# Transposes moved ahead of filler matmuls, and key and value tiles that rotate singly over seven PSUM banks, in a one-core hybrid block

## The reference

```python
t = t + _L2_ffn_ref(_ln_t(t), router_w, router_b, expert_w, expert_b)   # mixture of experts
t = t + _L3_attn_ref(_ln_t(t), mask, wq_w, wq_b, wk_w, wk_b, ...)       # linear attention, 16 heads of 32
t = t + _L3_ffn_ref(_ln_t(t), sigma, phi, M_u, ...)                     # spectral layer
```

## Time and profile before

| | us |
|---|---|
| median of 3 runs | 213.16 |
| lowest and highest run | 212.28 and 216.89 |
| span of the profiled execution | 211.0 |
| its busy time, PE | 179.3 |
| its busy time, DVE | 154.0 |
| its busy time, ACT | 97.4 |

### The profile page before, as it was taken

The page is one execution under the profiler, slowest core; times in us unless marked ns, Lnnn a source line. Parts: engine busy times, 40 slices in busy tenths (PEclk is TensorE's granted clock), DMA queues, the critical chain, the costliest instruction groups (busy, mean ns, idle before and its releaser), DMA issues.

```text
span 211.0 us, 7008 instructions
## 1 busy us (share of the span) xinstructions
PE 179.3 (85%) x3059; PEld 132.5 (63%) x3067; DVE 154.0 (73%) x347; ACT 97.4 (46%) x240; POOL 39.2 (19%) x57
## 2 busy tenths in 40 slices
PE   7799989798999987993688899768589979978994
PEld 2677669798998987931234677325245827646872
DVE  2789998959899999969877455598668757647201
ACT  2743998386889869422011351120758620016200
POOL 5971000004404413450100300332100000120000
PEclk9999999999999999999999999999965899999999
DMA  6930346344457530000044021001210072000000
GB/s 185 289 118 5 89 151 199 102 158 149 151 160 207 158 95 0 7 1 2 10 155 123 20 65 55 0 0 28 69 33 0 6 173 45 0 0 3 3 0 25
DMA packets 9203, 16.03 MB, mean 76 GB/s; under 512 B 2536, under 2 KB 3912, under 8 KB 9044
## 3 DMA queue, kind: packets, MB, share of 16 engines
q1 hardware_dynamic: 9028, 15.28, 24.4%
q10 hardware_dynamic: 144, 0.30, 0.4%
HBM read 15.15 MB, written 0.42 MB: 74 GB/s over the span
## 4 chain that ended last, share of the span: by engine, by line
PE 48%; DVE 32%; issue 8%; ACT 7%; POOL 2%; DMA 2%; POOLq 1%; DVEq 0%
PE ps L1547 46%; DVE onehot L1075 5%; DVE dots L1101 2%; POOL rstd L583 2%; DVE arena L455 2%; DMA cst<-in_cst 2%; DVE att L1125 1%; DVE arena L440 1%; ACT arena L646 1%; DVE stu_fq L1450 1%; ACT onehot L842 1%; ACT table L646 1%; ACT arena L863 1%; ACT arena L730 1%; DVE dots L1107 1%
## 5 line engine op out<-in xcount | busy, mean ns | idle before, releaser
L1547 PE MATMUL ps<-table,onehot 128*128 128x64 bf16 x1728 | 52.4, 193 | 5.6 <-DVE onehot L1075 2.9
L1547 PEld LDWEIGHTS ps<-table,onehot 128*128 128x128 bf16 x1728 | 51.3, 98 | 6.9 <-issue 4.0
L1547 PE MATMUL ps<-spare 128*128 128x512 bf16 (+1 forms) x120 | 31.4, 385 | 9.8 <-DVE rexp L1366 2.3
L730 ACT ACTIVATE arena<-ps 128x512 f32<-128x512 f32 (+1 forms) x40 | 21.3, 553 | 13.8 <-PE ps L1547 13.7
L455 POOL TENSOR_TENSOR arena<-arena,w4p 128x288 f32<-128x288 f32 x21 | 16.2, 802 | 58.2 <-DVE arena L455 58.0
L1547 PEld LDWEIGHTS ps<-spare 128*128 128x128 bf16 x128 | 11.2, 102 | 22.9 <-issue 2.8
L583 POOL TENSOR_TENSOR rstd<-var_eps,cst 128x4 f32<-128x4 f32 (+2 forms) x9 | 8.8, 982 | 80.5 <-DVE var_eps L944 54.6
L1547 PE MATMUL ps<-arena 128*32 128x66 f32 (+6 forms) x388 | 22.1, 277 | 0.2 <-DVE arena L1327 0.2
L646 ACT ACTIVATE arena<-ps 128x512 f32<-128x512 f32 (+4 forms) x17 | 7.2, 465 | 31.2 <-PE ps L1547 25.5
L1547 PEld LDWEIGHTS ps<-arena 128*32 128x32 f32 (+3 forms) x388 | 18.3, 146 | 4.3 <-issue 1.6
L1075 DVE TENSOR_SCALAR onehot<-indexb,cst 128x2304 bf16<-128x2304 bf16 (+1 forms) x24 | 17.7, 770 | 0.0
(11 more groups left out here) (280 smaller groups left out, 306.9 us busy)
## 6 DMA issues: line engine op xcount, KB each, us to landing
indexb<-index_rows SPq DMA_DIRECT2D x20, 288.0 KB, 3.5
stu_fq<-index_rows SPq DMA_DIRECT2D x8, 288.0 KB, 3.4
arena<-in_toep SPq DMA_DIRECT2D x2, 514.0 KB, 5.9
l<-in_l SPq DMA_DIRECT2D x1, 646.5 KB
stu_fq<-in_stu SPq DMA_DIRECT2D x1, 560.0 KB, 3.7
onehot<-in_l3w SPq DMA_DIRECT2D x1, 512.0 KB
table<-stu_mixed SPq DMA_DIRECT2D x4, 128.0 KB, 2.2
l<-in_l SPq DMA_DIRECT2D x1, 384.0 KB, 7.0
```

Of the source, the lines that this page charges most:

```text
L730: nc.scalar.activation(gv[:, b % 2, :, at:at + count, :], ps[:, SB[n % len(SB)], 0:count * SLOT].rearrange("p (s a d) -> p a s d", s=count ...
L1547: return nc.tensor.matmul(out_ap, lhsT, rhs, start=start, stop=stop)
```

## The change

Mixture: the four fillers behind `eps1` go, and each half is turned, copied and multiplied before the next half is turned, with one filler behind each transpose. The wait for the expert weights' load moves ahead of the first transpose.

Linear attention: the three fillers behind `x41` and the three behind `cen1` go; two fillers with no wait of their own stand ahead of the first transpose. Bank 0 (`ROWBANK`) holds both transposes. The sixteen key and value tiles rotate over the other seven banks in the order in which they are read, so `v3` takes the bank that `fk0` frees, `k4` that of `vs0`, `v4` that of `fk1`, and so on: each waits for a single step. `turn1` comes right behind `v2`, and its copy `rows1` stands on ACT behind `vc0`. `queries(0)` waits for no step for image 0, and for `vs4`, `fk5`, `vs5` for the others.

```diff
-        t4 = Steps(sem("tensor_moe"), "turn0 turn1 experts0 experts1 sum")
+        t4 = Steps(sem("tensor_moe"), "turn0 experts0 turn1 experts1 sum")
...
-        a5 = Steps(sem("scalar_linear"), "rows0 ek0 vc0 ek1 vc1 ek2 vc2 ek3 rows1 vc3 " + " ".join(f"ek{t} vc{t}" for t in range(4, T))
+        a5 = Steps(sem("scalar_linear"), "rows0 ek0 vc0 rows1 " + " ".join(f"ek{t} vc{t}" for t in range(1, T))
...
-        t5 = Steps(sem("tensor_linear"), "turn0 k0 k1 k2 k3 v0 v1 v2 v3 turn1 k4 k5 v4 v5 k6 k7 v6 v7"
+        t5 = Steps(sem("tensor_linear"), "turn0 k0 k1 k2 k3 v0 v1 v2 turn1 v3 k4 v4 k5 v5 k6 v6 k7 v7"
...
-        KBANK, VBANK = (lambda t: 2 * t % 8), (lambda t: (2 * t + 1) % 8)
+        KBANK, VBANK, ROWBANK = (6, 1, 3, 5, 7, 2, 4, 6), (7, 2, 4, 6, 1, 3, 5, 7), 0
...
-                if t == 3:
-                    rows_copied(t5, a5, 1, VBANK(0))
                 act.wait_ge(t5.sem, t5[f"v{t}"])
...
+                if t == 0:
+                    rows_copied(t5, a5, 1, ROWBANK)
...
             occupied_after(v3, ("x3", 4), bank=6)
-            occupied_after(v4, ("var0", 4), ("eps1", 4), bank=6)
-            turned_rows(v4, t4, 0, 4)
-            occupied(1, 6)
-            turned_rows(v4, t4, 1, 5)
+            occupied_after(v4, ("var0", 4), bank=6)
             pe.wait_ge(d_moe, 5 * 16)
             for h in range(NH):
+                turned_rows(v4, t4, h, 4 + h)
+                occupied(1, 6)
                 pe.wait_ge(a4.sem, a4[f"rows{h}"])
...
-            tile_biases(range(B), KBANK, WK, stop=False)
-            occupied_after(v4, ("x41", 3), bank=7)
+            tile_biases(range(B - 1), KBANK, WK, stop=False)
+            pe.wait_ge(v4.sem, v4["x41"])
+            tile_biases([B - 1], KBANK, WK, stop=False)
             tile_biases(range(B - 1), VBANK, WV, stop=False)
-            occupied_after(v5, ("cen1", 3), bank=7)
-            turned_rows(v5, t5, 0, 7)
+            occupied(2, ROWBANK)
+            turned_rows(v5, t5, 0, ROWBANK)
             pe.wait_ge(a5.sem, a5["rows0"])
             tile_products("k", range(B), KBANK, WK, start=False)
-            tile_biases([B - 1], VBANK, WV, stop=False)
-            tile_products("v", range(B), VBANK, WV, start=False)
-            pe.wait_ge(v5.sem, v5["vs0"])
-            turned_rows(v5, t5, 1, VBANK(0))
-            for pair in ((4, 5), (6, 7)):
-                for name, bank, w, freed in (("k", KBANK, WK, "fk"), ("v", VBANK, WV, "vs")):
-                    pe.wait_ge(v5.sem, v5[f"{freed}{pair[1] - 4}"])
-                    if name == "v" and pair[0] == 4:
-                        pe.wait_ge(a5.sem, a5["rows1"])
-                    tile_biases(pair, bank, w, stop=False)
-                    pe.wait_ge(a5.sem, a5["rows1"])
-                    tile_products(name, pair, bank, w, start=False)
+            tile_products("v", range(B - 1), VBANK, WV, start=False)
+            turned_rows(v5, t5, 1, ROWBANK)
+            for name, t, freed in (("v", 3, "fk0"), ("k", 4, "vs0"), ("v", 4, "fk1"), ("k", 5, "vs1"), ("v", 5, "fk2"),
+                                   ("k", 6, "vs2"), ("v", 6, "fk3"), ("k", 7, "vs3"), ("v", 7, "fk4")):
+                bank, w = (KBANK, WK) if name == "k" else (VBANK, WV)
+                pe.wait_ge(v5.sem, v5[freed])
+                tile_biases([t], bank, w, stop=False)
+                pe.wait_ge(a5.sem, a5["rows1"])
+                tile_products(name, [t], bank, w, start=False)
...
-                        if g == 0:
-                            pe.wait_ge(v5.sem, v5[f"fq{b}" if pair else f"vs{B + b // 2}"])
+                        if g == 0 and (pair or b):
+                            pe.wait_ge(v5.sem, v5[f"fq{b}" if pair else ("vs4", "fk5", "vs5")[b - 1]])
```

More of the change, by code:

```diff
@@ L856, in _ @@
             nc.scalar.activation(rexp[:], rexp[:], ACT.Exp).then_inc(a4.sem, a4.step("rexp"))
-            rows_copied(t5, a5, 0, 7)
+            rows_copied(t5, a5, 0, ROWBANK)
             for t in range(T):
@@ L862, in _ @@
                 act.wait_ge(t5.sem, t5[f"k{t}"])
-                nc.scalar.activation(fk[:, t * BANK:(t + 1) * BANK], ps[:, KBANK(t), :], ACT.Exp, bias=neg1[:])\
+                nc.scalar.activation(fk[:, t * BANK:(t + 1) * BANK], ps[:, KBANK[t], :], ACT.Exp, bias=neg1[:])\
                     .then_inc(a5.sem, a5.step(f"ek{t}"))
-                if t == 3:
-                    rows_copied(t5, a5, 1, VBANK(0))
                 act.wait_ge(t5.sem, t5[f"v{t}"])
-                copy(vcv[:, t, :, :, 0:D], ps[:, VBANK(t), :].rearrange("p (g r n) -> p g r n", g=HG, r=4), a5, f"vc{t}",
+                copy(vcv[:, t, :, :, 0:D], ps[:, VBANK[t], :].rearrange("p (g r n) -> p g r n", g=HG, r=4), a5, f"vc{t}",
                      c["cs"][:, 2 * h:2 * h + 1])
+                if t == 0:
+                    rows_copied(t5, a5, 1, ROWBANK)
             def heads_copied(hg):
@@ L1440, in _ @@
                 dve.wait_ge(a5.sem, a5[f"ek{t}"])
-                nv.scalar_tensor_tensor(out=fk[:, blk], in0=fk[:, blk], scalar=1.0, in1=ps[:, KBANK(t), :],
+                nv.scalar_tensor_tensor(out=fk[:, blk], in0=fk[:, blk], scalar=1.0, in1=ps[:, KBANK[t], :],
                                         op0=ALU.min, op1=ALU.max).then_inc(v5.sem, v5.step(f"fk{t}"))
                 dve.wait_ge(a5.sem, a5[f"vc{t}"])
-                nv.tensor_scalar(vcv[:, t, :, :, D:2 * D], ps[:, VBANK(t), :].rearrange("p (g r n) -> p g r n", g=HG, r=4),
+                nv.tensor_scalar(vcv[:, t, :, :, D:2 * D], ps[:, VBANK[t], :].rearrange("p (g r n) -> p g r n", g=HG, r=4),
                                  c["cs"][:, 2 * h + 1:2 * h + 2], None, ALU.mult).then_inc(v5.sem, v5.step(f"vs{t}"))
@@ L1876, in tile_biases @@
                     bias = BIAS[t % B]
-                    ins = biased(ps[:, bank(t), :], bias, lin_b[bias, w], **kw)
+                    ins = biased(ps[:, bank[t], :], bias, lin_b[bias, w], **kw)
                 return ins
@@ L1883, in tile_products @@
                     b, rows = IMAGES[t % B]
-                    mm(ps[:, bank(t), :], half_of(ln_rows, t // B)[rows, :], lin_w[rows, w], **kw)\
+                    mm(ps[:, bank[t], :], half_of(ln_rows, t // B)[rows, :], lin_w[rows, w], **kw)\
                         .then_inc(t5.sem, t5.step(f"{name}{t}"))
-            tile_biases(range(B), KBANK, WK, stop=False)
-            occupied_after(v4, ("x41", 3), bank=7)
+            tile_biases(range(B - 1), KBANK, WK, stop=False)
+            pe.wait_ge(v4.sem, v4["x41"])
+            tile_biases([B - 1], KBANK, WK, stop=False)
             tile_biases(range(B - 1), VBANK, WV, stop=False)
-            occupied_after(v5, ("cen1", 3), bank=7)
-            turned_rows(v5, t5, 0, 7)
+            occupied(2, ROWBANK)
+            turned_rows(v5, t5, 0, ROWBANK)
             pe.wait_ge(a5.sem, a5["rows0"])
             tile_products("k", range(B), KBANK, WK, start=False)
-            tile_biases([B - 1], VBANK, WV, stop=False)
-            tile_products("v", range(B), VBANK, WV, start=False)
-            pe.wait_ge(v5.sem, v5["vs0"])
-            turned_rows(v5, t5, 1, VBANK(0))
-            for pair in ((4, 5), (6, 7)):
-                for name, bank, w, freed in (("k", KBANK, WK, "fk"), ("v", VBANK, WV, "vs")):
-                    pe.wait_ge(v5.sem, v5[f"{freed}{pair[1] - 4}"])
-                    if name == "v" and pair[0] == 4:
-                        pe.wait_ge(a5.sem, a5["rows1"])
-                    tile_biases(pair, bank, w, stop=False)
-                    pe.wait_ge(a5.sem, a5["rows1"])
-                    tile_products(name, pair, bank, w, start=False)
+            tile_products("v", range(B - 1), VBANK, WV, start=False)
[7 more added lines that the diff above has]
+                tile_products(name, [t], bank, w, start=False)
             def queries(pair):
```

## The result

Over 20 runs of each, the changed kernel takes 211.69 us in the median (210.11 to 213.67), the kernel before 213.73 (211.82 to 216.89). The ratio is 0.9919, with a 95% interval of 0.9892 to 0.9945: faster by 0.8%, which is less than the 2% line. Every ratio in this document leaves out the slow runs, those over 1.5% above the fastest of their kernel, so it is not the quotient of the medians. The forecast was 210.5 in a range of 208.6 to 212.6.

The account below looks back on a forecast made before the run. DVE was taken to set most of the pace, with PE setting it in three places and starving DVE in the tile loop. From 213.16 us, 4.1 gained less 1.6 lost to the clock left 2.5: forecast 210.5, range 208.6 to 212.6.

Parts of the forecast that it names:

- The transposes: Mixture and linear attention: logits 0.78 us earlier, first key products 0.7 us more, together 1.5 us.
- the copy `rows1` on ACT: Linear attention: the copy moves behind `vc0` and delays later ACT steps, at most 0.28 us, taken as 0.1.
- The starved steps: Loop over tiles: single tiles over seven banks end DVE's waits of 0.48 and 1.45 us, saving 1.93 us.
- The clock falls in the loop: The forecast case: PE drops to 1.2 GHz among the single tiles, 1.6 of 4.1 us not seen, 210.5 us; chance 0.50.
- The price: Loop at the lower clock: key and value products come 0.2 to 1.5 us late, taken as 0.9.
- the wait before `fq0`: After the loop: query banks come free one by one, so DVE's 0.61 us wait before the first query feature goes.
- 0.7 for `kv0` and `kv1`: After the loop at the lower clock: they take up to 3.24 for 2.05 us; 0.7 of the 1.19 is lost.
- the rival of the full clock: The clock stays full through the tiles, so the whole 4.1 us is seen: 209.0 us; chance 0.27.
- this way to be wrong: Stated failure sign: the clock is down for longer than before, through `kv2`, `kv3` and the denominators.
- The sum: Whole change: 4.1 us gained at full clock, 1.6 us not seen at the lower clock, 2.5 us left.
- the tiles are not fed earlier: Rival: ACT or hand-overs pace the loop, DVE stays starved, only the transposes' 1.4 us count: 211.8 us; chance 0.13.
- Strict order: Rival: matmuls go strictly one behind another, single tiles lose overlap, `vs7` ends about 164.2, time 214.8 us; chance 0.10.

Follow-up runs that it names:

- half_columns: The changed kernel computing only half of the columns of the nine products from `v3` to `v7`; ratio to the kernel before 0.9868, four runs.
- query_images: The changed kernel with the first four query tiles issued image by image, both halves and biases of one image together; ratio to the kernel before 0.9941.
- spread_queries: The changed kernel with image 3's query tile in bank 0, mostly issued behind `v3`, other images one by one; ratio to before 0.9925, then 0.9951.

## Why the prediction was right within its range and 1.2 us too low

*The transposes.* Predicted 0.78 us for the logits: 0.71. Predicted 1.5 for the keys: 1.49 in the profile, and 5.1 and 15.8 in every profile of a kernel that has these edits. The second transposes, the moved wait for the weights and the copy `rows1` on ACT cost nothing that shows: DVE doesn't wait for the second logits, and its steps from `fk1` to `fk5` follow each other without a gap.

*The starved steps.* Predicted: 0.48 and 1.45 us go. They did. `vs7` was to end 2.6 us earlier, after the loss in the loop (1.5 - 0.1 + 1.93 + 0.2 - 0.9), and ended 2.52 earlier. The parts fit as well as the sum: 1.49 + 1.93 - 0.90 = 2.52.

*The clock falls in the loop.* Predicted at even chances: all three profiles of the changed kernel show it, at 149.6, 151.5 and 147.6 us. (The change puts in three fillers and not two: one more stands in the mixture, behind the second transpose.) The price was 0.9 (0.2 to 1.5): 0.90, 0.79, and 1.02 + 0.81 where it fell among the keys, which is outside that range. `half_columns` shows that it is PE's time. That the price was met to 0.01 is luck, as it was taken near the middle of a wide range.

*After the loop: the term that was mis-sized.* The prediction gave 0.61 us for the wait before `fq0` and took off 0.7 for `kv0` and `kv1`, in all 0.1 lost between the end of `vs7` and `eq4`. The 0.7 has a wrong base: it was taken from 3.24 against 2.05 us, but `kv0` and `kv1` took 3.24 us already in the kernel before, so by those rows a clock that is down again loses nothing there. That 0.7 lies near the 0.51 measured is luck. By the same slip the rival of the full clock was priced without the 1.19 us that it would gain there. It lost 2.52 - 1.16 = 1.36. The pieces: `kv0` starts 0.56 us behind the end of `vs7` in place of 0.06, since PE is still at image 3's queries at 1.2 GHz (0.50); it takes 3.75 in place of 3.24 us, as the clock is down through all of it (0.51); and the query products behind it take 1.06 us in place of 0.71 (0.35). The prediction let DVE's four query features cover a part of the longer `kv`. They cover nothing: `query_images` starts them 1.26 us earlier and `eq4` stays, so they weren't on the path. `spread_queries` takes the first piece away, and `kv0` then starts 0.06 us behind `vs7` again. The prediction did name this way to be wrong, a clock that is down for longer than before, though it placed the end of that at `kv2`; the clock came back at 163.3, ahead of `kv2`.

*The sum.* Predicted 4.1 - 1.6 = 2.5 us; 4.1 - 0.9 - (0.61 + 1.36) = 1.2 us is seen in the changed stretch of the first profiles. The ends of the other two profiles of the changed kernel lie 1.3 and 0.8 us ahead of that of the earlier trace rows, and 3.5 us or more ahead of the second profile of before. The medians differ by 2.04 us, between these. (The forecast was taken off the median of three runs, 213.16; over 20 runs it is 213.73, so 0.6 of the 1.2 us by which the forecast was low is that.) That the medians come nearer to 2.5 than the first profiles do is luck: the prediction has no term for falls of the clock ahead of the tiles. One candidate for the rest: of the three profiles with the mixture's old order two show a fall of the clock between 138 and 143 us and their keys start 1.5 us later than in the third; of the eleven with the new order none does. Three profiles are too few to call that shown.

*The rivals.* That the clock stays full didn't happen in a profile of the changed kernel. That the tiles are not fed earlier is excluded by the missing 0.48 and 1.45. Strict order would have ended `vs7` near 164.2 - 130.63 = 33.6; it ended at 29.15, and the rows from 152.32 show matmuls of several tiles in flight together. For the starts in this kernel that speaks against what the prediction cited beside this rival from the Trainium skill (TensorE: Matmul & The Clock Gate, Part 3, "What overlaps and what doesn't"), that matmuls start and end strictly in program order.

## What to carry to other kernels

A step that was starved and is now fed hands its gain to what stands behind it on the engine that feeds it: count that engine's work through to the next join (here PE to `kv1` and `q4`), at the clock that rows show for such work. A row priced at the lower clock may be at that clock in the kernel before already, as `kv0` and `kv1` were here; compare it with itself. Before reading a gain from two spans, measure both from a row ahead of the change; here more than half of the difference lay ahead of it. Take two profiles of the kernel before, too; here they differ by more than the first pair gave for the change. And a wait that one edit removes without moving the next landmark (`fq0` here) was never worth its idle column.

## What the runs showed of the hardware

The clock's falls are not the same from one execution of a kernel to the next. Eleven of the fourteen profiles show it down near 100 us and six near 131, both in code that is the same in all, and two of the three with the mixture's old order show it down at about 140. Over the 76 executions of the kernel before that ran beside the experiments, the mean granted clock was at most 0.976, and the span follows it: 210.1 us in the mean of the 18 at 0.976, 212.1 of the 23 at 0.960, 214.5 of the 13 at 0.936. This spread of over 4 us is larger than any edit tried here.

In the changed kernel PE was busy for 2.00 of 2.00 us in each window from 150 to 158 us, with products on 32 rows and their biases, and the clock stayed at 0.50. It came back at 163.3, behind the 3.75 us of work on all 128 rows that begin at 158.84 and during the query products on 32 rows that follow. What makes it fall at one moment and not at another was not settled.
